# An AdaLN + routed FFN kernel: the gate's products moved between the up product and the latents

## The chip, the cores and the metric

One core of a Trainium2 chip runs the kernel. The metric is the device time in microseconds (us) of one launch, as the median of several runs.

## What is computed

There are 64 sequences of 32 channels with 512 features (2048 tokens of 512). A small network turns each sequence's condition into a mixture of 8 kernels, which mixes the 32 channels; then comes a feed-forward block with a shared path and a routed path, a layer norm, and the residual.

```python
h   = einsum('boi,bih->boh', agg_w, x) + agg_b[:, :, None]      # mix of the channels
logits = h @ gate_w                                              # 512 -> 8
routing_weights, _ = top_k(logits, 2)
shared = (relu(h @ up_w) ** 2) @ down_w                          # 512 -> 1024 -> 512
x_latent = h @ fc1_w                                             # 512 -> 256
routed = ((x_latent @ expert_w) * sum(routing_weights)) @ fc2_w  # 256 -> 512
out = x + layernorm(shared + routed) * gamma + beta
```

## The kernel before

The 2048 tokens are worked in 4 blocks of 512 (TB = 4 tiles of 128). Block 0 is written out (its weights are still being split), blocks 1 and 2 are a loop, block 3, the last, is written out. Features lie on the partitions and tokens along the free dimension, so the products up to the down product use the weights as the stationary or moving side of 128x128x512 products.

To keep fp32 accuracy at the faster fp32r rate, a value is split in a high part (fp32r) and a low part (the rest), and each product is done as three: high x high, high x low, low x high (`three_products`, L933 to L935). ScalarE makes the high parts by a copy, VectorE the low parts by a subtraction. The gate's product (L1000) and the channel mix (L908) are plain fp32 products; one of those is two instructions in the trace.

TensorE's order in a block (`block_of`, L1046): the up product (8 columns of 128, 12 products each), the latents (`latent_product`, 2 x 12 products, `lc` = 0, 1), the gate (16 small products of 8 columns, four at a time side by side in the array), then the mix of the next block (four chunks of 4 products), except in the last block, and the down product, tile by tile (`down_product`: 6 products of the routed path, 24 of the shared one). In the last block the down product follows the gate directly. The weights expert_w and fc2_w are folded into one matrix q ahead of block 0.

PSUM has 8 banks. The up columns go through banks 0 to 3 in turn, the latents into banks 0 and 1, the gate into bank 2, the mix's chunks into banks 3, 5, 7 and 0. So the gate waits for the relu that empties bank 2 (column 6, L994), and the mix's fourth chunk waits for the first latent's low half (L1068). The down product's first tile waits for the high and the low half of each latent (L1028, L1029).

The engines work in order, each through its own list of instructions, and hand over by semaphores that count up. ScalarE in a block: relu and square of the 8 up columns (L514, L516), then `latent_gate` (L518: the two latent copies L521, then the gate's logits copied to `gate_rows`, L523), then the high parts of the next block's h (L472) and the scaling of the routed tiles (L531). VectorE: the two halves of each square (L687, L689), `latent_low` (L695), the first two bias sums of the next block's h (L631), `top_two` (L698: one 32x32-wise transposition, four maxima of 8, one sum), the low parts of h (L662), and the layer norm of the four tiles. In block 0 both also split the weights (L536 and L766 for down_w, L467 and L626 for q), so they run behind. GpSimd builds the next block's mixing matrices and takes the inverse deviation; SyncE loads x and stores tiles.

Of the kernel before, what the change touches and what calls it, by code (L numbers as in the profile page):

```python
# [5 lines left out]
def adaln_ffn_kernel(  # L6
# [43 lines left out]
    G = P // C  # L50
# [3 lines left out]
    NBLK = NT // TB  # L54
# [24 lines left out]
    with ctx:  # L79
        def sb(name, shape, dt=fp32):  # L80
            return ctx.enter_context(nc.sbuf_tensor(name, shape, dt))

        def sem(name):
            return ctx.enter_context(nc.semaphore(name))
# [88 lines left out]
        gate_rows = sb("gate_rows", [P, TB, C])  # L173
# [15 lines left out]
        GATE = ps[:, GATE_BANK, 0:P].rearrange("p (t r) -> p t r", t=TB)  # L189
# [77 lines left out]
        fc1_lo_ready = sem("fc1_lo_ready")  # L267
# [19 lines left out]
        gate_done = sem("gate_done")  # L287
        gate_copied = sem("gate_copied")
# [145 lines left out]
        def _(act):  # L434
# [81 lines left out]
                nc.scalar.activation(relu_sq[:, m % 2, :], relu_sq[:, m % 2, :], ACT.Square).then_inc(square_done, 1)  # L516

            def latent_gate(b):  # L518
                for lc in range(LC):
                    act.wait_ge(lat_done, LC * b + lc + 1)  # L520
                    nc.scalar.copy(lat_hi[:, lc, :], ps[:, LAT_BANK[lc], :]).then_inc(lat_hi_ready, 1)  # L521
                act.wait_ge(gate_done, G * (b + 1))
                nc.scalar.copy(gate_rows[:, :, :], GATE).then_inc(gate_copied, 1)  # L523

            def scale_routed(b, tiles=TB):
                act.wait_ge(top2_done, b + 1)
# [11 lines left out]
            for m in range(IC):  # L538
# [6 lines left out]
                if m in (6, 7):  # L545
                    q_high(m - 6)
            latent_gate(0)
            mix_high(1)
            scale_routed(0)
# [18 lines left out]
        def _(dve):  # L568
# [55 lines left out]
            def q_low(lc):  # L624
                dve.wait_ge(q_hi_ready, lc + 1)
                nc.vector.tensor_tensor(q_lo[:, lc, :], Q[lc], q_hi[:, lc, :].bitcast(fp32),  # L626
                                        ALU.subtract).then_inc(q_lo_ready, 1)

            def mix_bias(b, c):
                dve.wait_ge(mix_done, HC * b + c + 1)  # L630
                nc.vector.tensor_tensor(h_sum[c], ps[:, MIX_BANK[c], :],  # L631
                                        agg_b[:, bass.ds(b * TOK, TOK)], ALU.add).then_inc(h_ready, 1)
# [23 lines left out]
            def sum_aggregate(b):  # L656
                dve.wait_ge(next_terms_ready, b + 1)
                nc.vector.tensor_reduce(agg[:, bass.ds((b + 1) * TB, TB), :], next_terms, AX.X, ALU.add).then_inc(next_agg_ready, 1)
# [26 lines left out]
            def split_square(b, m):  # L685
                dve.wait_ge(square_done, IC * b + m + 1)
                nc.vector.tensor_copy(sq_hi[:, m, :], relu_sq[:, m % 2, :]).then_inc(sq_hi_ready, 1)  # L687
                dve.wait_ge(sq_hi_ready, IC * b + m + 1)
                nc.vector.tensor_tensor(sq_lo[:, m, :], relu_sq[:, m % 2, :], sq_hi[:, m, :].bitcast(fp32),  # L689
                                        ALU.subtract).then_inc(sq_lo_ready, 1)  # L690

            def latent_low(b):
                for lc in range(LC):
                    dve.wait_ge(lat_hi_ready, LC * b + lc + 1)
                    nc.vector.tensor_tensor(lat_lo[:, lc, :], ps[:, LAT_BANK[lc], :],  # L695
                                            lat_hi[:, lc, :].bitcast(fp32), ALU.subtract).then_inc(lat_lo_ready, 1)

            def top_two(b):  # L698
                dve.wait_ge(gate_copied, b + 1)
                nc.vector.transpose(logits[:, :, :].rearrange("p t e -> p (t e)"),  # L700
                                    gate_rows[:, :, :].rearrange("p t r -> p (t r)")).then_inc(gate_turned, 1)
                dve.wait_ge(latents_loaded, 16)
                dve.wait_ge(gate_turned, b + 1)
                for t in range(TB):
                    nc.vector.max(out=top8[:, t, :], in_=logits[:, t, 0:NE]).then_inc(top8_done, 1)
                dve.wait_ge(top8_done, TB * (b + 1))
                nc.vector.tensor_tensor(top2[:, :], top8[:, :, 0], top8[:, :, 1], ALU.add).then_inc(top2_done, 1)
# [91 lines left out]
            q_low(0)  # L799
            split_square(0, 7)  # L800
            q_low(1)
            latent_low(0)
            dve.wait_ge(aggb_loaded, 16)
            mix_bias(1, 0)
            mix_bias(1, 1)
            top_two(0)
            mix_low(1, 0)
            mix_bias(1, 2)
            mix_low(1, 1)
# [5 lines left out]
            with dve.Fori(1, NBLK - 1) as b:  # L815
                for m in range(IC):
                    split_square(b, m)
                    if m == 3:
                        spread_aggregate(b)
                    if m == 4:  # L820
                        sum_aggregate(b)
                latent_low(b)
                mix_bias(b + 1, 0)
                mix_bias(b + 1, 1)
                top_two(b)
                mix_low(b + 1, 0)
                mix_bias(b + 1, 2)
                mix_low(b + 1, 1)
                mix_bias(b + 1, 3)
                mix_low(b + 1, 2)  # L830
                mix_low(b + 1, 3)
                for t in range(TB):
                    normalise(b, t)
            for m in range(IC):
                split_square(NBLK - 1, m)
            latent_low(NBLK - 1)
            top_two(NBLK - 1)
            dve.wait_ge(spread_copied, 1)
            for lc in range(LC):
                nc.vector.tensor_tensor(lat_scaled[:, lc, :], ps[:, LAT_BANK[lc], LAST], spread_sb,  # L840
# [10 lines left out]
        def _(pe):  # L851
# [120 lines left out]
            def up_product(b):  # L972
                for m in range(IC):
                    if m >= WB:
                        pe.wait_ge(relu_done, IC * b + m - WB + 1)
                    for c in range(HC):
                        if m == 0:
                            pe.wait_ge(h_hi_ready, HC * b + c + 1)
                            pe.wait_ge(h_lo_ready, HC * b + c + 1)
                        last = up_chunk(m, c)  # L980
                    last.then_inc(up_done, 1)

            def latent_product(b):
                for lc in range(LC):
                    cols = slice(lc * P, (lc + 1) * P)
                    pe.wait_ge(relu_done, IC * b + WB + lc + 1)
                    for c in range(HC):
                        last = three_products(ps[:, LAT_BANK[lc], :], fc1_hi[:, c, cols], fc1_lo[:, c, cols],
                                              h_hi[:, c, :], h_lo[:, c, :], c == 0, c == HC - 1)
                    last.then_inc(lat_done, 1)  # L990

            def gate_product(b):

                pe.wait_ge(relu_done, IC * b + WB + LC + 1)  # L994
                pe.wait_ge(h_kept, HC)
                last = [None] * G
                for c in range(HC):
                    tokens = h_sum[c].rearrange("p (t q r) -> p q t r", q=G, r=C)
                    for q in range(G):
                        last[q] = nc.tensor.matmul(ps[q * C:q * C + NE, GATE_BANK, 0:P], gate_raw[:, c, :],  # L1000
                                                   tokens[:, q, :, :], start=(c == 0), stop=(c == HC - 1),
                                                   tile_position=(0, q * C))
                for q in range(G):
                    last[q].then_inc(gate_done, 1)
# [41 lines left out]
            def block_of(b, first_block=False, last_block=False):  # L1046
                if first_block:
                    up_first_block()
                    pe.wait_ge(fc1_lo_ready, 1)
                else:  # L1050
                    up_product(b)
                latent_product(b)
                gate_product(b)
                if not last_block:

                    pe.wait_ge(x_loaded, 16 * (b + 2))
                    pe.wait_ge(mix_ready, G * (b + 1))
                    pe.wait_ge(relu_done, IC * (b + 1))
                    mix_chunk(b + 1, 0, MIX_BANK[0])
                    if first_block:  # L1060
                        pe.wait_ge(h_lo_ready, HC - 1)
                    else:
                        pe.wait_ge(y_done, TB * b)
                    mix_chunk(b + 1, 1, MIX_BANK[1])
                    if first_block:
                        pe.wait_ge(q_lo_ready, LC)
                    mix_chunk(b + 1, 2, MIX_BANK[2])
                    pe.wait_ge(lat_lo_ready, LC * b + 1)  # L1068
                    mix_chunk(b + 1, 3, MIX_BANK[3])
                down_product(b, first_block, last_block)  # L1070
# [54 lines left out]
```

## Time and profile before

| what | us |
|---|---|
| median of 3 runs | 257.05 (256.86 to 257.37) |
| the profiled execution | 257.08 |
| its span, first to last instruction | 255.3 |
| TensorE busy (products) | 248.5 |
| TensorE weight loads | 207.7 |
| VectorE busy | 155.9 |
| ScalarE busy | 81.7 |
| GpSimd busy | 39.6 |

PE in the rows is TensorE's products, PEld its weight loads, which overlap with them; DVE is VectorE, ACT ScalarE, POOL GpSimd. Products are pipelined: one of 128x512 lasts 0.39 us in its row, but the next starts 0.23 us after it. L12 is line 12 of the kernel. A wait is shown as the idle time ahead of an instruction with the instruction that ended it.

### The profile page before, as it was taken

The numbers are of one execution on the slowest core, as the hardware profiler recorded it, in microseconds if no ns is written. First come the engines' busy times: TensorE is split into PE (matmuls) and PEld (weight loads), VectorE is DVE, ScalarE is ACT, GpSimd is POOL, SyncE is SP. The second block draws the span as 40 slices with busy tenths as digits, with TensorE's granted clock in tenths as the row PEclk, the third lists the DMA queues.
The fourth block names the chain that finished last, engine by engine and source line by source line (L and its number), as shares of the span: only waits on it lengthen the run. The fifth ranks groups of instructions, "written<-read, shape, count | busy, mean of one in ns | idle before, by whom it ended". The sixth has DMA issues, their size and how long they took to land.

```text
span 255.3 us, 3527 instructions
## 1 busy us (share of the span) xinstructions
PE 248.5 (97%) x1293; PEld 207.7 (81%) x1293; DVE 155.9 (61%) x272; ACT 81.7 (32%) x141; POOL 39.6 (16%) x46
## 2 busy tenths in 40 slices
PE   8999999999999999999999999999999999999992
PEld 7778887988888888888888888888888888788891
DVE  4798999844448964544447984464444963406453
ACT  4569865320013353321111544331111355202100
POOL 2400021001116220001113401001111700001110
PEclk9999999999999999999999999999999999999999
DMA  5992804001111400001110220000111100000211
GB/s 142 355 366 101 307 13 156 0 0 44 41 41 41 163 4 0 3 0 42 41 41 33 68 104 0 0 0 0 41 41 44 42 0 0 3 0 5 77 44 41
DMA packets 10428, 15.60 MB, mean 61 GB/s; under 512 B 1072, under 2 KB 4912, under 8 KB 10416
## 3 DMA queue, kind: packets, MB, share of 16 engines
q1 hardware_dynamic: 9968, 15.33, 17.2%
q8 instruction: 8, 0.13, 0.2%
q10 hardware_dynamic: 448, 0.11, 0.2%
q14 instruction: 4, 0.03, 0.0%
HBM read 11.23 MB, written 4.20 MB: 60 GB/s over the span
## 4 chain that ended last, share of the span: by engine, by line
PE 91%; issue 3%; DMA 2%; DVE 2%; ACT 0%; POOL 0%; SPq 0%; POOLq 0%; DVEq 0%
PE ps L933 28%; PE ps L935 27%; PE ps L934 27%; PE ps L908 4%; DMA experts_sb<-in_experts_dram 2%; PE ps L1000 2%; PE ps L861 2%; PE ps L914 1%; POOL rstd L419 0%; DVE h_lo L642 0%; DVE stats L716 0%; DVE y_buf L714 0%; DVE h_full L638 0%; ACT h_hi L476 0%; POOLq L79 0%
## 5 line engine op out<-in xcount | busy, mean ns | idle before, releaser
L933 PE MATMUL ps<-down_hi,sq_hi 128*128 128x512 f32 (+1 forms) x136 | 51.2, 377 | 0.0
L934 PE MATMUL ps<-down_lo,sq_hi 128*128 128x512 f32 (+1 forms) x136 | 51.2, 377 | 0.0
L935 PE MATMUL ps<-down_hi,sq_lo 128*128 128x512 f32 (+1 forms) x136 | 51.2, 377 | 0.0
L933 PE MATMUL ps<-h_hi,up_hi 128*128 128x512 f32 x126 | 49.1, 390 | 0.2 <-DVE h_lo L642 0.2
L935 PE MATMUL ps<-h_hi,up_lo 128*128 128x512 f32 x126 | 49.1, 389 | 0.0
L934 PE MATMUL ps<-h_lo,up_hi 128*128 128x512 f32 x126 | 49.0, 389 | 0.0
L419 POOL TENSOR_TENSOR rstd<-mv,half 128x1 f32<-128x1 f32 x16 | 15.3, 955 | 158.8 <-DVE mv L721 153.8
L514 ACT ACTIVATE relu_sq<-ps 128x512 f32<-128x512 f32 x32 | 19.1, 597 | 57.6 <-PE ps L935 45.6
L714 DVE TENSOR_TENSOR y_buf<-ps,y_buf 128x512 f32<-128x512 f32 x15 | 10.4, 692 | 41.0 <-PE ps L935 40.7
L687 DVE CAST sq_hi<-relu_sq 128x512 fp32r<-128x512 f32 x32 | 22.6, 705 | 16.3 <-ACT relu_sq L516 15.7
L934 PEld LDWEIGHTS ps<-down_lo,sq_hi 128*128 128x128 f32 x136 | 25.6, 188 | 4.7
L933 PEld LDWEIGHTS ps<-down_hi,sq_hi 128*128 128x128 f32 x136 | 25.6, 188 | 4.7
L935 PEld LDWEIGHTS ps<-down_hi,sq_lo 128*128 128x128 f32 x136 | 25.6, 188 | 4.6
L531 ACT ACTIVATE y_buf<-ps,top 128x512 f32<-128x512 f32 x15 | 10.2, 687 | 56.7 <-PE ps L935 56.7
L933 PEld LDWEIGHTS ps<-h_hi,up_hi 128*128 128x128 f32 x126 | 23.7, 188 | 5.5 <-DVE h_lo L642 0.6
L935 PEld LDWEIGHTS ps<-h_hi,up_lo 128*128 128x128 f32 x126 | 23.7, 188 | 4.9
L934 PEld LDWEIGHTS ps<-h_lo,up_hi 128*128 128x128 f32 x126 | 23.7, 188 | 4.9
L689 DVE TENSOR_TENSOR sq_lo<-relu_sq,sq_hi 128x512 fp32r<-128x512 f32 x32 | 26.5, 827 | 1.1
L516 ACT ACTIVATE relu_sq<-relu_sq 128x512 f32<-128x512 f32 x32 | 20.2, 633 | 1.0
L729 DVE SCALAR_TENSOR_TENSOR late<-y_buf,rstd,late 128x512 f32<-128x512 f32 x15 | 11.3, 751 | 7.6 <-POOL rstd L419 5.6
L412 POOL TENSOR_TENSOR late<-x_cur,affine_sb 128x2048 f32<-128x2048 f32 x3 | 14.2, 4741 | 2.8 <-DVE late L729 2.8
L933 PE MATMUL ps<-q_hi,lat_hi 128*128 128x512 f32 (+1 forms) x34 | 13.3, 390 | 0.0
(137 smaller groups left out, 299.7 us busy)
## 6 DMA issues: line engine op xcount, KB each, us to landing
out_dram<-late SPq DMA_DIRECT2D x15, 256.0 KB, 2.0
x_cur<-in_x_dram SPq DMA_DIRECT2D x3, 1024.0 KB, 5.5
late<-in_down_w_dram SPq DMA_DIRECT2D x4, 512.0 KB, 5.1
late<-in_up_w_dram SPq DMA_DIRECT2D x3, 512.0 KB, 8.2
x_cur<-in_x_dram SPq DMA_DIRECT2D x2, 512.0 KB, 6.4
agg_b<-aggb_dram SPq DMA_DIRECT2D x1, 768.0 KB, 5.9
latents_sb<-in_latents_dram SPq DMA_DIRECT2D x1, 528.0 KB, 5.3
experts_sb<-in_experts_dram SPq DMA_DIRECT2D x1, 512.0 KB, 5.1
```

The costliest lines, as they stand in the source:

```text
L412: nc.gpsimd.tensor_tensor(x_beta, x_cur[:, :, :], beta_b.unsqueeze(1).to_broadcast([P, TB, HID]), ALU.add).then_inc(xbeta_ready, 1)
L419: nc.gpsimd.tensor_tensor(rstd[:, :], mv[:, 1:2], half[:, :], ALU.pow).then_inc(rstd_done, 1)
L514: nc.scalar.activation(relu_sq[:, m % 2, :], ps[:, UP_BANK[m], :], ACT.Relu).then_inc(relu_done, 1)
L516: nc.scalar.activation(relu_sq[:, m % 2, :], relu_sq[:, m % 2, :], ACT.Square).then_inc(square_done, 1)
L687: nc.vector.tensor_copy(sq_hi[:, m, :], relu_sq[:, m % 2, :]).then_inc(sq_hi_ready, 1)
L689: nc.vector.tensor_tensor(sq_lo[:, m, :], relu_sq[:, m % 2, :], sq_hi[:, m, :].bitcast(fp32), ALU.subtract).then_inc(sq_lo_ready, 1)
L714: nc.vector.tensor_tensor(y, shared(t), y, ALU.add).then_inc(y_done, 1)
L729: nc.vector.scalar_tensor_tensor(out=out_buf[:, t, :], in0=y, scalar=rstd[:, :], in1=x_beta[:, t, :], op0=ALU.mult, op1=ALU.add).then_inc( ...
L908: last = nc.tensor.matmul(ps[:, bank, t * P:(t + 1) * P], x_cur[:, t, c * P:(c + 1) * P], mix[:, t, :], start=True, stop=True)
L933: nc.tensor.matmul(dst, a_hi, b_hi, start=first, stop=False)
L934: nc.tensor.matmul(dst, a_hi, b_lo, start=False, stop=False)
L935: return nc.tensor.matmul(dst, a_lo, b_hi, start=False, stop=last)
```

## The change

On TensorE the gate's 16 products move from behind the latents to between the up product and the latents, in all four blocks; the wait for fc1_lo, which block 0 made ahead of both, is made behind the gate. On ScalarE the copy of the logits moves ahead of the two latent copies. On VectorE the ranking (`top_two`) moves ahead of `latent_low`; in blocks 0 to 2 this also takes it from between the bias sums and the low parts of h. No instruction is added or removed.

```diff
             def latent_gate(b):
+                act.wait_ge(gate_done, G * (b + 1))
+                nc.scalar.copy(gate_rows[:, :, :], GATE).then_inc(gate_copied, 1)
                 for lc in range(LC):
                     act.wait_ge(lat_done, LC * b + lc + 1)
                     nc.scalar.copy(lat_hi[:, lc, :], ps[:, LAT_BANK[lc], :]).then_inc(lat_hi_ready, 1)
-                act.wait_ge(gate_done, G * (b + 1))
-                nc.scalar.copy(gate_rows[:, :, :], GATE).then_inc(gate_copied, 1)
@@ block 0 on VectorE
             q_low(1)
+            top_two(0)
             latent_low(0)
             dve.wait_ge(aggb_loaded, 16)
             mix_bias(1, 0)
             mix_bias(1, 1)
-            top_two(0)
             mix_low(1, 0)
@@ blocks 1 and 2 on VectorE
+                top_two(b)
                 latent_low(b)
                 mix_bias(b + 1, 0)
                 mix_bias(b + 1, 1)
-                top_two(b)
                 mix_low(b + 1, 0)
@@ last block on VectorE
+            top_two(NBLK - 1)
             latent_low(NBLK - 1)
-            top_two(NBLK - 1)
             dve.wait_ge(spread_copied, 1)
@@ TensorE
             def latent_product(b):
+                if isinstance(b, int) and b == 0:
+                    pe.wait_ge(fc1_lo_ready, 1)
                 for lc in range(LC):
@@
                 if first_block:
                     up_first_block()
-                    pe.wait_ge(fc1_lo_ready, 1)
                 else:
                     up_product(b)
+                gate_product(b)
                 latent_product(b)
-                gate_product(b)
                 if not last_block:
```

## Rows read from the trace of the kernel before

**Rows 1.** The page: busy us by engine, and TensorE's granted clock in 40 slices.

```profile
PE 248.5 (97%) x1293; PEld 207.7 (81%) x1293; DVE 155.9 (61%) x272; ACT 81.7 (32%) x141; POOL 39.6 (16%) x46
...
PEclk9999999999999999999999999999999999999999
```

**Rows 2.** TensorE's waits: line, releaser; us in total, times, longest.

```profile
PE ps L855 <- DVE warm L570: 1.1, 1, 1.1
...
PE ps L861 <- DMA experts_sb<-in_experts_dram: 0.2, 1, 0.2
```

**Rows 3.** Timeline, block 0's up product: start, us, instruction, idle before and releaser.

```profile
16.92 0.68 DVE L642 TENSOR_TENSOR h_lo<-h_full,h_hi 128x512 fp32r<-128x512 f32 x1
...
17.66 0.50 PE L933 MATMUL ps<-h_hi,up_hi 128*128 128x512 f32 x1 [0.21 <-DVE h_lo L642]
...
17.99 0.39 PE L934 MATMUL ps<-h_lo,up_hi 128*128 128x512 f32 x1
```

**Rows 4.** Timeline of TensorE, block 1: latents, gate, mix, down.

```profile
97.36 0.39 PE L933 MATMUL ps<-h_hi,fc_hi 128*128 128x512 f32 x1
...
102.58 0.39 PE L935 MATMUL ps<-h_hi,fc_lo 128*128 128x512 f32 x1
102.89 0.62 PE L1000 MATMUL ps<-h_full,latents_sb 128*8 128x128 f32 x16
...
103.89 3.84 PE L908 MATMUL ps<-mix,x_cur 128*128 128x128 f32 x32
107.48 0.48 PE L933 MATMUL ps<-q_hi,lat_hi 128*128 128x512 f32 x1
```

**Rows 5.** Timeline, last block: last latent product, gate, start of down.

```profile
220.92 0.39 PE L935 MATMUL ps<-h_hi,fc_lo 128*128 128x512 f32 x1
...
221.24 0.62 PE L1000 MATMUL ps<-h_full,latents_sb 128*8 128x128 f32 x16
221.35 0.59 ACT L521 CAST lat_hi<-ps 128x512 fp32r<-128x512 f32 x1 [2.13 <-PE ps L935]
...
221.97 0.69 DVE L695 TENSOR_TENSOR lat_lo<-ps,lat_hi 128x512 fp32r<-128x512 f32 x1 [2.03 <-ACT lat_hi L521]
...
222.23 0.50 PE L933 MATMUL ps<-q_hi,lat_hi 128*128 128x512 f32 x1
...
222.57 0.40 PE L934 MATMUL ps<-q_lo,lat_hi 128*128 128x512 f32 x1
...
222.75 0.31 DVE L700 STREAM_TRANSPOSE logits<-gate_rows 128x128 f32<-128x128 f32 x1
222.81 0.39 PE L935 MATMUL ps<-q_hi,lat_lo 128*128 128x512 f32 x1
...
223.03 0.40 PE L933 MATMUL ps<-q_hi,lat_hi 128*128 128x512 f32 x1
...
223.27 0.39 PE L934 MATMUL ps<-q_lo,lat_hi 128*128 128x512 f32 x1
...
223.57 0.17 DVE L707 TENSOR_TENSOR top<-top 128x4 f32<-128x4 f32 x1
```

**Rows 6.** Timeline, a lone split product among the first mix's products.

```profile
13.19 0.48 PE L925 MATMUL ps<-sq_lo 128*128 128x512 f32 x1
13.27 0.42 PEld L914 LDWEIGHTS ps<-mix,x_cur 128*128 128x128 f32 x2
...
13.50 0.27 PE L914 MATMUL ps<-mix,x_cur 128*128 128x128 f32 x1
```

**Rows 7.** Timeline of ScalarE, block 1: relu of up column 6.

```profile
94.84 0.60 ACT L514 ACTIVATE relu_sq<-ps 128x512 f32<-128x512 f32 x1 [1.46 <-PE ps L935]
```

**Rows 8.** Timeline, block 0: relu of up column 6, last up product.

```profile
37.44 0.60 ACT L514 ACTIVATE relu_sq<-ps 128x512 f32<-128x512 f32 x1 [2.28 <-DVE sq_lo L689]
...
37.96 0.39 PE L935 MATMUL ps<-h_hi,up_lo 128*128 128x512 f32 x1
```

**Rows 9.** Timeline of VectorE, block 0: low half of q ahead of the latents'.

```profile
43.52 0.68 DVE L626 TENSOR_TENSOR q_lo<-ps,q_hi 128x512 fp32r<-128x512 f32 x1
```

## The prediction

> **What bounds the kernel now.** I read the page first: TensorE is busy 248.5 of 255.3 us at its full clock of 2.4 GHz (tenths of 9 in every slice) [rows 1]. Then the list of what TensorE waited for: four entries, the first and the last of which stand in [rows 2], 1.9 us in all. The latest in time is the wait for h_lo (L642), at 17.6 us, in the first block's up product [rows 3]. So from there to its last product the array never stands still for another engine, and each us put between two of its products is a us of the result. What ScalarE and VectorE do counts only where it makes TensorE wait. Hence two questions, answered from the timelines around the moved work: does the new order cost the array more by itself, and is one of its waits now met too late?
>
> The profiled execution took 257.08 us, 255.3 of it span and 1.8 around it; the median of the runs is 257.05. I add to 257.08 and take the result as the median's.
>
> **Part 1: the array's own time, blocks 0 to 2.** Nothing is added: the gate's 16 products (32 instructions) stay, in another place. What can change is the cost of switching between the split products (fp32r, 512 columns) and the plain fp32 ones (gate and mix). Before, a block runs up, latents, gate, mix, down: two switches. After, it runs up, gate, latents, mix, down: four. In block 1 the 24 latent products start from 97.36 to 102.58, one in 0.227 us; the gate starts 0.31 after the last of them (102.89), and the mix 1.00 after the gate (103.89) [rows 4]. So from the last up product to the first of the mix it is 24 x 0.227 + 0.31 + 1.00 = 6.76 us. After, the gate starts 0.31 behind the last up product. The step from gate to a split product is shown in the last block, which has no mix: 221.24 to 222.23 is 0.99, then 0.34 to the second product and 0.24 to the third [rows 5]. Then 21 steps of 0.227 to the last latent product (4.77), and the step from a split product into the mix: the trace has one place where a lone split product (L925) stands among the first mix's products, and the next of them starts 0.31 after it [rows 6]. Sum: 0.31 + 0.99 + 0.34 + 0.24 + 4.77 + 0.31 = 6.96 us, so **+0.20 us a block, +0.6 us for three**.
>
> Bounds: if the step into the mix costs no more than a plain slot (0.227 instead of 0.31) and the slow start behind the gate is absent (0.12 less), nothing is left; if a 128-column load, 0.2 us (two of them take 0.42 in L914's row [rows 6]), were uncovered at the step into the mix, it is some 0.35 to 0.4 a block. I use 0.0 to 1.0 us for the three, and 0.6 since each of its steps has a row of its own.
>
> A rule of the Trainium skill bears on that upper end: in "TensorE: Matmul & The Clock Gate", section "LDWEIGHTS (loading the stationary operand)", a weight load's time goes by its columns, one in a cycle of 1.2 GHz. By it the mix's 128 columns would cost about 0.1 us more at a switch than the gate's 8, where nothing covers them, and Part 1 would be about 0.9 us (an estimate from that page). The row of L914 behind L925 speaks against it: its load starts at 13.27, while L925 (from 13.19, 0.48 us long) still runs [rows 6].
>
> **Part 2: the gate's own waits.** The gate writes bank 2, so it waits for the relu of up column 6 (L994, relu_done 7). In block 1 that relu ends at 94.84 + 0.60 = 95.44 [rows 7], and the gate would start at 97.45. In block 0 ScalarE is behind, held up by VectorE: the relu runs from 37.44 to 38.04 [rows 8]. The last up product starts at 37.96 [rows 8], so the gate would start at 38.27, and the relu is 0.23 us ahead. Price 0; if the queue stops for it all the same, about one slot, 0.2 us. Behind this wait stand the latents and so all of TensorE. The wait for fc1_lo goes behind the gate and costs nothing: the same latents started unwaited one slot after 37.96 in before [rows 2].
>
> **Part 3: the latents' halves against the mix, blocks 0 to 2.** The latents now end right before the mix. The chain behind their last product is, in block 3: product at 220.92, ScalarE's copy from 221.35, VectorE's low half 221.97 to 222.66, so 1.74 us from the product's start [rows 5]. After, the mix starts 0.31 behind that product and takes 3.59 us (103.89 to 107.48) [rows 4]; the down product needs this half only then, 3.9 us behind it. Cover 2.2 us, no wait. The mix's fourth chunk overwrites bank 0 and needs the first low half, and the ranking now stands ahead of that on VectorE: transposition, four maxima and sum take 1.0 us (222.75 to 223.74) [rows 5]. The worst is block 0, where VectorE is busy with q_lo until 44.20 [rows 9]: ranking to 45.2, first low half to 45.9, second to 46.6. The last latent product is then at 37.96 + 0.31 + 0.99 + 0.34 + 0.24 + 4.77 = 44.61, the mix starts at 44.92, its fourth chunk 2.7 us later at 47.6, down at 48.5. Both are met with over 1.5 us. Queued behind on VectorE are the next block's bias sums, which start some 0.4 us later in block 0; but the low halves of h behind them come sooner, as the ranking is out of their way, and the down product first asks for these sums at its second tile, 30 products (6.8 us) on. On ScalarE the copy of the logits stands ahead of the latents' copies; it waits for a gate that is done before the last square is. The next x load hangs on the end of the mix (SyncE and GpSimd wait for it) and moves by the 0.2 us of Part 1. All this I put at 0. Nor is anything gained: the routing sums come sooner, but TensorE waits for none [rows 2].
>
> **Part 4: the last block.** It has no mix. Before, the gate's 1.0 us stood between the latents and the down product and hid much of the 1.74 us chain: the second low half was there at 222.66, and the first product that needs it (lc = 1) started at 223.03, 0.37 us later [rows 5]. Now the gate stands ahead. The last up product is 24 slots ahead of 220.92, at 215.48; so the last latent product is at 215.48 + 0.31 + 0.99 + 0.34 + 0.24 + 4.77 = 222.13 (+1.2, without Part 1's shift). VectorE is free: it stood idle 2.03 us before the second low half [rows 5], and the ranking, 1.0 us, goes in ahead of the first one, between gate and latents. Second low half: 222.13 + 1.74 = 223.87. Meanwhile the array has three products on the first half, from 222.35 to 223.03, and then waits. The one like wait in the trace shows the restart: h_lo ends at 16.92 + 0.68 = 17.60, the product starts at 17.66 and the next 0.33 later [rows 3]. So the lc = 1 products come at 223.92 and 224.25, where they came at 223.03 and 223.27 [rows 5]: **+0.97 us**. Everything behind is array-bound to its last product, and the tail keeps its form, so it goes through whole. Bounds: 0.75 (restart at a plain slot, a chain 0.1 shorter) to 1.2 us (each step of the chain a little longer, the next 0.5 later, as long as L933's row behind that wait [rows 3]).
>
> **Sum.** 257.08 + 0.60 + 0 + 0 + 0.97 = **258.65 us**, +0.6%.
>
> **Rivals.** (a) *The last block's chain stays covered*, and the result is not slower. Its place is the lc = 1 wait, and it decides if the second low half is there within 0.9 us (four slots) of the last latent product. For it: ScalarE and VectorE are idle there. Against: the product's own 0.39, the copy's 0.59 and the subtraction's 0.69 us in a row [rows 5]. With Part 1 as computed it gives 257.7; with a third of it, 257.3. Chance 0.07. (b) *The array gains*, because the gate costs less behind up than between latents and mix: its 1.31 us from latents to mix become one plain slot, and the gate's fixed costs go under the up product. If 0.3 us fell away in each of three blocks, and (a) held, it is 257.08 - 0.9 = 256.2. No row shows such a thing; 0.02. (c) *Block 0's gate waits too*, for a relu later than 38.27 or a queue that stopped (0.2), and the mix's load is uncovered (3 x 0.15): 258.65 + 0.65 = 259.3; 0.12. The forecast itself: 0.79.
>
> **How the numbers follow.** What can be told from no change here is 0.2%, 0.5 us. Slower: forecast and (c), 0.91, and the part of (a) at 257.7, 0.01: 0.92. Same: the rest of (a), 0.06. Faster: (b), 0.02. Range: low 257.08 + 0.1 + 0.75 = 257.9; high 257.08 + 1.0 + 0.1 + 1.2 = 259.4.
>
> **What would show it.** After the change: one new TensorE wait, on VectorE's lat_lo, of some 0.6 to 0.9 us at about 224; 6.96 us from last up to first mix product; products at 0.34 and 0.24 behind the gate; block 0's gate at 38.27; no other wait. If the 6.96 is still 6.76, Part 1 is wrong; if the wait is missing, Part 4; if block 0's gate starts late, Part 2. A time under 257.6 would mean that the last block hides its chain in a way these rows don't show.

## The result, and the profile after

The changed kernel takes 258.28 us (median of 22 runs, 257.86 to 260.42), the kernel before in the same rounds 257.35 us (22 runs, 256.74 to 259.27). The ratio is 1.0044, with an interval of 1.0027 to 1.0060: slower by 0.44%, some 1.1 us (0.93 us between the two medians), beyond the 0.2% that can be told from no change. The profiled execution took 258.25 us, 256.4 of it span, against 257.08 and 255.3. The forecast was slower, at 258.65 in a range of 257.9 to 259.4; the time lies in it.

TensorE's list of waits has one new entry, the second line here, and the entry of 0.2 us on experts_sb in the start-up is gone (line, releaser; us in total, times, longest):

```profile
PE ps L855 <- DVE warm L570: 1.1, 1, 1.1
PE ps L933 <- DVE lat_lo L695: 0.8, 1, 0.8
PE ps L950 <- ACT h_hi L476: 0.4, 1, 0.4
PE ps L933 <- DVE h_lo L642: 0.2, 1, 0.2
```

It stands in the last block, where the forecast put it. Timeline of TensorE, last block, last up product to down (the answer to [rows 5]):

```profile
215.54 0.39 PE L935 MATMUL ps<-h_hi,up_lo 128*128 128x512 f32 x1
215.86 0.62 PE L1002 MATMUL ps<-h_full,latents_sb 128*8 128x128 f32 x16
...
216.85 0.50 PE L933 MATMUL ps<-h_hi,fc_hi 128*128 128x512 f32 x1
217.19 0.40 PE L934 MATMUL ps<-h_lo,fc_hi 128*128 128x512 f32 x1
...
222.19 0.39 PE L935 MATMUL ps<-h_hi,fc_lo 128*128 128x512 f32 x1
222.42 0.39 PE L933 MATMUL ps<-q_hi,lat_hi 128*128 128x512 f32 x1
...
222.87 0.39 PE L935 MATMUL ps<-q_hi,lat_lo 128*128 128x512 f32 x1
224.08 0.47 PE L933 MATMUL ps<-q_hi,lat_hi 128*128 128x512 f32 x1 [0.82 <-DVE lat_lo L695]
224.38 0.40 PE L934 MATMUL ps<-q_lo,lat_hi 128*128 128x512 f32 x1
```

The chain of work that ended last now leaves TensorE there, for ScalarE's copy and VectorE's subtraction, and comes back (start, us, what):

```profile
222.62 0.59 ACT lat_hi L523
223.21 0.03 issue
223.24 0.70 DVE lat_lo L695
223.94 0.14 issue
224.08 0.47 PE ps L933
```

Three products on the first latent end their slots at 223.10, and nothing else is let in until 224.08. From the last up product to the second of lc = 1 it is 224.38 - 215.54 = 8.84 us. Before, it was 223.27 - 215.48 = 7.79: the 223.27 is in [rows 5], and the last up product of before is this row:

```profile
215.48 0.39 PE L935 MATMUL ps<-h_hi,up_lo 128*128 128x512 f32 x1
```

The difference is 1.05 of the 1.1 us by which the span grew.

The other three blocks, in TensorE's timeline of block 1 (the answer to [rows 4]):

```profile
97.14 0.39 PE L935 MATMUL ps<-h_hi,up_lo 128*128 128x512 f32 x1
97.46 0.62 PE L1002 MATMUL ps<-h_full,latents_sb 128*8 128x128 f32 x16
...
103.79 0.39 PE L935 MATMUL ps<-h_hi,fc_lo 128*128 128x512 f32 x1
104.02 3.73 PE L908 MATMUL ps<-mix,x_cur 128*128 128x128 f32 x32
107.51 0.48 PE L933 MATMUL ps<-q_hi,lat_hi 128*128 128x512 f32 x1
```

The mix's weight loads start while the product at 103.79 still runs (TensorE's weight loads):

```profile
103.80 3.77 PEld L908 LDWEIGHTS ps<-mix,x_cur 128*128 128x128 f32 x32
```

The last up product of this block in before starts at the same time:

```profile
97.14 0.39 PE L935 MATMUL ps<-h_hi,up_lo 128*128 128x512 f32 x1
```

Last up product to mix: 104.02 - 97.14 = 6.88 us, where it was 103.89 - 97.14 = 6.75. But mix to down: 107.51 - 104.02 = 3.49, where it was 3.59 [rows 4]. Together it is 10.37 against 10.34, in each of blocks 0 to 2: the two more switches cost 0.03 us a block, not 0.20.

### The profile page after: what moved, and what is told of

Read it like the earlier page. It is cut to its first block, busy times and chain, and to the rows that moved or that the text cites. A ratio compares the mean times of both kernels' runs of the same rounds, so it can differ in the third digit from the quotient of the medians.

```text
span 256.4 us, 3527 instructions
## 1 busy us (share of the span) xinstructions
PE 249.0 (97%) x1293; PEld 208.0 (81%) x1293; DVE 155.6 (61%) x272; ACT 81.3 (32%) x141; POOL 39.5 (15%) x46
## 4 chain that ended last, share of the span: by engine, by line
PE 93%; issue 3%; DVE 2%; ACT 1%; POOL 0%; POOLq 0%; DVEq 0%
PE ps L933 28%; PE ps L934 27%; PE ps L935 27%; PE ps L908 4%; PE ps L1002 2%; PE ps L861 1%; PE ps L855 1%; PE ps L914 1%; PE ps L883 0%; POOL rstd L419 0%; DVE h_lo L642 0%; DVE stats L716 0%; DVE y_buf L714 0%; DVE lat_lo L695 0%; DVE h_full L638 0%
```

## The experiments

Start-up of the kernel varies between profiled executions by more than these effects: the product that ends the wait for h_lo started at 17.66 in before [rows 3], and between 17.00 and 19.43 in the others. So beside the medians I give the stretch from that product to the start of the row that holds VectorE's last instructions, for each profiled execution: 234.46 us in before (17.66 to 252.12), 235.63 in the changed kernel (17.62 to 253.25), 1.17 more.

| kernel | median us | before, same rounds | stretch, us | against before |
|---|---|---|---|---|
| e1_last_back | 257.17 | 256.92 | 234.56 | +0.10 |
| e2_last_only | 257.91 | 256.92 | 235.55 | +1.09 |
| e3_tensor_only | 257.99 | 256.92 | 235.63 | +1.17 |
| e4_side_only | 260.73 | 256.92 | 238.31 | +3.85 |
| e5_cover_one | 257.63 | 257.03 | 234.92 | +0.46 |
| e6_cover_two | 257.14 | 257.03 | 234.55 | +0.09 |
| e7_gate_twice | 261.3 (one run) | 257.03 | 239.34 | +4.88 |
| after_again | 258.15 | 257.03 | 235.63 | +1.17 |
| e8_side_last | 260.73 | 256.82 | 236.69 | +2.23 |
| e9_gate_between | 258.26 | 256.82 | 235.66 | +1.20 |
| e10_side_again | 260.64 | 256.82 | 236.72 | +2.26 |

**Undo the last block.** The theory: all of the loss is one wait in the last block. The edit to the changed kernel, with the same swap back on ScalarE and VectorE in that block:

```diff
+                if last_block:
+                    latent_product(b)
+                    gate_product(b)
+                else:
-                gate_product(b)
-                latent_product(b)
+                    gate_product(b)
+                    latent_product(b)
```

> The changed kernel, but the last block in the order of before (latents, gate, down; logits copied and ranked after the latents' halves). Theory (the loss is one wait of TensorE in the last block, the switches in blocks 0 to 2 cancel out): TensorE's wait on lat_lo is gone, and the time is that of before plus 3 x 0.03 = 0.1 us, within 0.2 us. Rival 1 (the new order costs the array 0.20 us in each of blocks 0 to 2, as I had predicted): before plus 0.6 us. Rival 2 (the loss is spread, or comes with the moved copies and ranking in all blocks): most of the 1.1 us stays.

Measured: ratio 1.0004 (0.9982 to 1.0027), 0.25 us over before by the medians, 0.10 in the stretch. The wait is gone, and blocks 0 to 2 keep the 10.37 us of the changed kernel. The 0.6 us for switches, my own Part 1, would be a ratio of 1.0023 and so lies inside the interval; it is the stretch, where it would be six times what was measured, that makes it fall.

**Change the last block alone.** The mirror image, from the kernel before.

> The kernel before, but the last block alone in the changed order on all three engines. Theory (one wait in the last block): before plus 1.05 us, with a TensorE wait of 0.8 us on lat_lo near 224. Rival 1 (0.2 us a block for switches): before plus 0.5 us less than the changed kernel, so some 0.5 to 0.6. Rival 2 (spread over the blocks): about a quarter of the loss, 0.3 us.

Measured: ratio 1.0040 (1.0019 to 1.0061), 0.99 us by the medians, 1.09 in the stretch. The wait, and the restart behind it, are those of the changed kernel (TensorE's timeline):

```profile
222.44 0.39 PE L942 MATMUL ps<-q_hi,lat_lo 128*128 128x512 f32 x1
223.65 0.47 PE L940 MATMUL ps<-q_hi,lat_hi 128*128 128x512 f32 x1 [0.81 <-DVE lat_lo L702]
223.95 0.39 PE L941 MATMUL ps<-q_lo,lat_hi 128*128 128x512 f32 x1
```

0.10 and 1.09 add to 1.19; the whole change measured 1.17. The loss has its place.

**TensorE's move alone.** `latent_gate` and the calls of `top_two` are as in the kernel before; only `block_of` and `latent_product` are changed.

> TensorE's order changed in all blocks, ScalarE's and VectorE's left as before. Theory (only the latents' chain behind the last latent product counts, and the copy and the ranking are beside it in either place): the same as the changed kernel, before plus 1.1 us, with the same wait of 0.8 us. Rival (the ranking and the copy, moved, take part in the loss): less than 1.1 us, down to 0.5. If the early copy and ranking had shortened something, it would be over 1.3.

Measured: ratio 1.0035 (1.0015 to 1.0054), 1.07 us by the medians, 1.17 in the stretch, as the changed kernel to 0.01. So the copy and the ranking play no part in the loss, nor do they give anything back: ranked early or late, TensorE does not wait for it.

**ScalarE's and VectorE's order alone.** TensorE as before; on the other two the gate's logits are ahead of the latents.

> ScalarE's and VectorE's order changed (logits copied and ranked ahead of the latents' halves), TensorE's left as before (latents, gate). In the last block the latents' copies now queue behind the gate's: gate copy from 222.45 to 222.72, latent copies to 223.3 and 223.9, ranking to 223.74, first low half to 224.4, so the down product starts at 224.55 instead of 222.23. Theory: before plus 2.3 us, in one TensorE wait at the down product's first product; in blocks 0 to 2 the mix covers it (first low half 0.5 us ahead of the mix's fourth chunk). Rival (cover in blocks 0 to 2 is thinner than I read): up to 0.5 us a block more, 3 to 4 us in all.

Measured: ratio 1.0112 (1.0072 to 1.0152), from six runs: 258.89 and 259.01, and four from 260.58 to 261.11. The wait came where and as long as computed (TensorE's timeline), but the profiled execution was 3.85 us longer in its stretch, not 2.3. The products behind the wait show why:

```profile
224.52 0.47 PE L933 MATMUL ps<-q_hi,lat_hi 128*128 128x512 f32 x1 [2.18 <-DVE lat_lo L695]
224.83 0.39 PE L934 MATMUL ps<-q_lo,lat_hi 128*128 128x512 f32 x1
225.06 0.57 PE L935 MATMUL ps<-q_hi,lat_lo 128*128 128x512 f32 x1
225.43 0.63 PE L933 MATMUL ps<-q_hi,lat_hi 128*128 128x512 f32 x1
225.86 0.63 PE L934 MATMUL ps<-q_lo,lat_hi 128*128 128x512 f32 x1
...
228.42 0.44 PE L934 MATMUL ps<-down_lo,sq_hi 128*128 128x512 f32 x1
228.70 0.40 PE L935 MATMUL ps<-down_hi,sq_lo 128*128 128x512 f32 x1
```

From 225.06 to 228.42 they are 0.43 us apart (the first step 0.37) instead of 0.23, and the table of stretches gives the granted clock (the column ahead of the last two: 0.52, then 1.00; stretch, its us, busy us of five engines, PEclk, DMA share, GB/s):

```profile
225.00:228.50 3.50, 3.50 (x10) 2.69 (x10) 0.00 (x0) 0.00 (x0) 0.00 (x0) 0.52 0.02 5
228.50:232.00 3.50, 3.50 (x17) 2.87 (x16) 0.00 (x0) 0.00 (x0) 0.00 (x0) 1.00 0.00 0
```

So TensorE ran at 1.2 GHz there; ahead of it lay the gate's 1 us of small products and 2.18 us of idling. Ten products instead of 17 fit in 3.5 us: seven slots of 0.227, 1.6 us. That leaves 2.25 of the 3.85 for the wait. The rival (thin cover in blocks 0 to 2) was not seen: no wait stands in these blocks, and from the last up product to the down product each of them takes 10.34 us, as before. In block 1 VectorE's ranking ran from 104.44 and the down product started at 107.52 (before: 107.48).

**The same in the last block alone.**

> The kernel before, with ScalarE's and VectorE's order changed in the last block only (logits copied and ranked ahead of the latents' halves, TensorE as before). Theory (in e4_side_only one TensorE wait of 2.2 us in the last block did it all, and where more was lost, 1.6 us, it was TensorE's clock at 1.2 GHz behind that wait): a time of either before plus 2.1 us, with the clock at 2.4 GHz throughout, or before plus 3.8, with products 0.43 us apart for some us behind the wait; nothing between. Rival (the rest of e4's loss comes from blocks 0 to 2): before plus 2.1 us and never 3.8.

Measured: ratio 1.0147 (1.0117 to 1.0178). The eight runs are 259.17 and 259.41, then 260.58 to 261.17, none between. The profiled execution was the one of 259.41; its stretch is 2.23 us longer, and its products behind the same wait of 2.18 us go on 0.23 apart (the first step 0.31) at a granted clock of 1.00:

```profile
224.58 0.47 PE L940 MATMUL ps<-q_hi,lat_hi 128*128 128x512 f32 x1 [2.18 <-DVE lat_lo L702]
224.89 0.40 PE L941 MATMUL ps<-q_lo,lat_hi 128*128 128x512 f32 x1
225.12 0.40 PE L942 MATMUL ps<-q_hi,lat_lo 128*128 128x512 f32 x1
225.36 0.39 PE L940 MATMUL ps<-q_hi,lat_hi 128*128 128x512 f32 x1
```

The wait is thus a price of 2.2 us each time, and the clock, in the profiled execution of e4_side_only, a further 1.6 us.

**Again, for the counts.**

> The kernel of e4_side_only again, for how often each of its two times comes and for a profile of the lower one, if one falls there. Theory: before plus 2.1 or plus 3.8 us, with the wait of 2.2 us in both; blocks 0 to 2 as before to within 0.1 us.

Measured: ratio 1.0136 (1.0105 to 1.0167), six runs, all from 260.45 to 261.11. With the two above, 16 of 20 executions have the higher time. The profiled one has it for another reason. Its stretch is 2.26 us longer than before and its clock is 1.00 behind the wait; the rest of its time lies in the start-up, where six of the plain products that fold the weights took 2.89 us in place of 1.56 (the chain of before has these six at 6.93), while the ten behind them took the 2.43 or 2.44 us of before:

```profile
7.11 2.89 PE L861 MATMUL ps<-experts_sb 128*128 128x256 f32 x6
9.79 0.63 PE L890 MATMUL ps<-att_tiles,sel 128*128 128x128 f32 x2
...
10.56 2.44 PE L861 MATMUL ps<-experts_sb 128*128 128x256 f32 x10
```

This too is the clock, though the table of stretches shows 1.00 there. The trace's own entries for the granted clock begin at 10.63 us in this execution, at 6.11 in before's and at 3.99 to 6.93 in the other eleven; for the time ahead of the first entry the table shows 1.00 for want of one, and so does the row of nines in [rows 1]. The slow products end where the entries begin, and before that they are 0.43 us apart instead of 0.22, the same factor of two as in e4_side_only. So the 1.2 GHz lasted about 4.5 us longer at the start, and the product behind h_lo came at 19.43 instead of 17.66.

Two different places of the lower clock, then, make an execution some 1.6 to 1.8 us longer. A time of that kind is also found without this change: of 97 executions of the kernel before, in all the rounds, 15 lie from 258.46 up and the rest under 257.9. None of those 15 was profiled. A mean clock is on record for 12 of them, and in 11 it is 0.998 or 0.999, where e4's fall of 3.4 us alone took it to 0.993; so those 11 had no such fall, and a late start of the higher clock, which the mean doesn't count, would fit them. That is argued, not shown. For the 16 above the mean (0.988 to 0.994) doesn't tell the two apart, since e10_side_again's own 0.994 comes from 2.9 us at the lower level behind its last product; how many of them had a fall behind the wait stays open.

**Cover the chain by other work.** If the loss is only the uncovered chain, products of the shared path between the two routed ones must take it away, by as much as they last. In the changed kernel, last block, first tile:

```diff
+                    early = 1 if last_block and t == 0 else 0
                     for lc in range(LC):
+                        if lc == 1:
+                            for m in range(early):
+                                pe.wait_ge(sq_lo_ready, IC * b + m + 1)
+                                three_products(shared(t), sq_hi[:, m, rows], sq_lo[:, m, rows],
+                                               down_hi[:, m, :], down_lo[:, m, :], m == 0, False)
...
-                    for m in range(IC):
+                    for m in range(early, IC):
```

> The changed kernel; in the last block's first tile, one triple of the shared product (3 products, 0.68 us) stands between the routed products of lc = 0 and lc = 1. Theory (the 0.98 us lost before lc = 1 is nothing but the latents' chain of 1.74 us left uncovered): the triple fills 0.68 of it, 0.3 us of loss stay, so 0.6 to 0.7 us under the changed kernel, before plus 0.45 us, with a wait of some 0.15 us left. Rival (the down product's start costs something of its own behind the latents, or the wait slides with the work): little change, before plus 1.1 us.

Measured: ratio 1.0035 (1.0008 to 1.0063), 0.60 us by the medians, 0.46 in the stretch, 0.71 under the changed kernel. Three products (0.68 us) bought 0.71. What is left is a gap of 0.52 us instead of 0.23 ahead of lc = 1:

```profile
223.22 0.39 PE L935 MATMUL ps<-down_hi,sq_lo 128*128 128x512 f32 x1
223.74 0.47 PE L933 MATMUL ps<-q_hi,lat_hi 128*128 128x512 f32 x1
224.05 0.40 PE L934 MATMUL ps<-q_lo,lat_hi 128*128 128x512 f32 x1
```

With `early = 2`:

> The same with two triples (6 products, 1.36 us) between lc = 0 and lc = 1. Theory: the chain is covered whole, no TensorE wait on lat_lo, before plus 0.1 us, within 0.2 us. Rival: as for one triple, before plus 1.1 us; or, if 0.2 us a block are lost to switches, before plus 0.6 us.

Measured: ratio 1.0009 (0.9984 to 1.0035), 0.11 us by the medians, 0.09 in the stretch: the time of before, with the gate still in its new place. No wait on lat_lo is left, and lc = 1 follows without a gap (224.13, then 224.36):

```profile
224.13 0.39 PE L935 MATMUL ps<-down_hi,sq_lo 128*128 128x512 f32 x1
224.36 0.39 PE L933 MATMUL ps<-q_hi,lat_hi 128*128 128x512 f32 x1
224.59 0.39 PE L934 MATMUL ps<-q_lo,lat_hi 128*128 128x512 f32 x1
```

It is no faster than before, and could not be: TensorE had no wait to lose.

> The changed kernel once more beside the two covers, for comparison on the same chip: before plus 1.1 us.

Measured beside these two: ratio 1.0037 (1.0015 to 1.0059), 1.12 us by the medians, 1.17 in the stretch.

**The gate's price by itself.** In the kernel before, the 16 gate products are done a second time behind up.

> The kernel before, with the gate's 16 products done a second time behind up in every block (the same values into the same bank, ahead of the real ones). It prices the gate in its new place with its old place still filled. Theory (the gate costs the array as much behind up as behind the latents, 0.31 + 0.99 + 0.12 of slow start - 0.23 = 1.19 us): before plus 4 x 1.19 = 4.8 us, and the mix behind the real gate still takes 3.59 us. Rival (behind up the gate is partly hidden): under 4.4 us. No wait on lat_lo.

Measured, in one run: 261.3 us, 4.3 above the median of before. But its start-up was 0.66 us shorter than that of before's profile (17.00 against 17.66), and in the stretch it is 4.88 us longer, 1.22 a block where 1.19 was expected. In TensorE's timeline of block 1 both gates are to be seen:

```profile
97.72 0.39 PE L935 MATMUL ps<-h_hi,up_lo 128*128 128x512 f32 x1
98.03 0.62 PE L1012 MATMUL ps<-h_full,latents_sb 128*8 128x128 f32 x16
...
104.69 0.62 PE L1000 MATMUL ps<-h_full,latents_sb 128*8 128x128 f32 x16
...
105.68 3.84 PE L908 MATMUL ps<-mix,x_cur 128*128 128x128 f32 x32
109.27 0.48 PE L933 MATMUL ps<-q_hi,lat_hi 128*128 128x512 f32 x1
```

Behind the real gate the mix takes 109.27 - 105.68 = 3.59 us, as in before; in e1_last_back, where the mix follows the latents, 107.56 - 104.08 = 3.48. So standing directly behind the gate costs the mix 0.1 us; by what means no run shows. A gate thus costs about 1.2 us in either place: the rival that it is partly hidden behind up falls.

**The gate between the two latents.** One more place, TensorE only.

> The gate between the two latent products in all blocks (side engines as before). Theory (what counts is what stands between the last latent product and the first product that needs its low half): nothing stands there in the last block, so the wait of 0.8 us is as in the changed kernel, and before plus 1.1 us; relus are further ahead, which gives nothing. Rival (it is the gate's place right behind up that costs): before plus less than 0.6 us.

Measured: ratio 1.0049 (1.0023 to 1.0075), 1.44 us by the medians, 1.20 in the stretch, with the wait on lat_lo at 0.81 us. What counts is that nothing stands behind the last latent, not where the gate went.

## Why the prediction was right

The mechanism was the one forecast: one new wait, on the second low half, in the last block, and no other. The number owes something to the width of the range, since one of its two terms was far too high, and something to the rounds: before itself took 257.35 in them, not the 257.08 that the sum starts from. From 257.08 the measured rise of 0.93 to 1.13 us would give 258.0 to 258.2, closer to the low end of 257.9 than to the forecast.

- **The bound** (a us between two products is a us of the result): right. In the changed kernel the added time between TensorE's products comes to 1.13 of the 1.17 us of the stretch.
- **Part 1**, +0.20 us a block: wrong in size, +0.03 measured. Its terms were 0.31, 0.99, 0.34 and 0.24 up to the third latent product, and those that the rows above show came so (97.14 to 97.46 is 0.32; in the last block 215.86, 216.85, 217.19). From last up to first mix product it was 6.88 us, against 6.96. Two things were mis-sized. The step from a split product into the mix was taken as 0.31 from the lone product L925; but that one itself came behind plain ones, and its 0.31 is the slow start behind them, which is in the row of every such first product. Here the mix follows a run of 24, and the step is 0.23 (103.79 to 104.02; in block 0 44.59 to 44.82). So going from split to plain products does not cost the extra 0.08 us by itself; it appears where the plain ones are the gate's, and whether their 8 columns or their four places in the array cause it is not shown. And the mix was taken at 3.59 in either place, while this is its time behind the gate. Behind a split product it is 3.49. The low end of my range for this part, 0, was nearer than the value I took; its high end, 1.0 for three blocks, was less than the 0.35 to 0.4 a block named for it (1.05 to 1.2). By the Trainium skill ("TensorE: Matmul & The Clock Gate", section "LDWEIGHTS (loading the stationary operand)") an uncovered load would have made it more. Here the load was covered: it starts at 103.80, under the product of 103.79 that lasts 0.39 us. No run here shows an uncovered one.
- **Part 2**, block 0's gate at 38.27 behind the relu: the gate started at 38.26, the relu ended at 37.41 + 0.60 = 38.01, and the step from the last up product (37.94) was 0.32. No wait, price 0.
- **Part 3**, the halves against the mix: no wait in blocks 0 to 2, as said. In block 0 the low halves ran from 44.98 to 46.33 against 45.2 to 46.6 computed, and the down product started at 48.31.
- **Part 4**, +0.97 us (0.98 by its own rows, 224.25 - 223.27): measured +1.05. The last latent product at 222.19 - 215.54 = 6.65 us behind the last up product (6.65 computed); chain 222.19 to 223.93, 1.74 (1.74); restart 0.14 to 0.15 us behind the low half instead of 0.05, the next product 0.30 later instead of 0.33. Nearly all of the 0.08 of difference is the restart.
- **The sum**: 0.08 + 1.05 = 1.13 where I had 0.60 + 0.97 = 1.57. The profiled execution came out 0.40 us under the forecast: Part 1 was 0.52 too high, Part 4 0.08 too low, and 0.04 of the stretch has no place of its own. Rivals (a) to (c) did not occur; e6_cover_two shows what (a) would have needed, two more triples between the latents and lc = 1.

## What to carry to other kernels

Where one engine never waits, moving its work changes little by itself (0.03 us a block here); look instead at what the moved work used to cover. Here the gate's 1.0 us stood, in the last block alone, between a producer chain of 1.74 us and its user, and a block without the mix is where that shows: read the peeled first and last blocks separately from the loop. A cost of switching read from one instruction that is itself behind a switch counts the same cost twice. And if a small piece of work has to move, a few independent products between producer and user (here six) give the time back.

## What the runs showed of the hardware that was not expected

Behind a TensorE wait of 2.18 us the clock fell in one profiled execution: the granted clock was 0.50 (1.2 GHz) from 0.6 us behind the end of the wait, for 3.4 us, which cost 1.6 us. In two others (e8_side_last, e10_side_again), with the same small gate products and the same wait ahead, it stayed at 2.4 GHz. The Trainium skill ("TensorE: Matmul & The Clock Gate", section "Why this matters for your kernels") warns of idle gaps between bursts of products that take the clock back to the lower level. The gaps it warns of are longer than this one: the first of these executions shows the lower level behind a shorter gap, the two others that a gap of this length need not bring it. The wait of 0.8 us was followed by full clock in all five profiled executions that had it.

Also, the start-up, up to the wait for h_lo and the same in all these kernels, varied by up to 2.4 us among the profiled executions (17.00 to 19.43). The latest of them is the one whose clock reached 2.4 GHz at 10.63 us, where the others did so by 6.93. So a comparison of stretches behind it told 0.1 us where the medians told 0.3.
